# Gated cross-attention block, one core: the opening's loads, bias sums and the place of the next contexts' statistics

## What is computed

```python
x = x + tanh(g_xattn) * attention(layernorm(x), ctx)   # own layer norms and affine gains inside
x = x + tanh(g_ffn) * ffn(layernorm(x))                # W1, W2 -> round(W / (mean|W| + 1e-5)) in {-1, 0, 1}
# attention(query, context):
q, c = layer_norm(query, gq, betq), layer_norm(context, gkv, betkv)
Q, K, V = q @ Wq + bq, c @ Wk + bk, c @ Wv + bv        # 16 heads
out = softmax(Q K^T * 32**-0.5) V @ Wo + bo
```

## Time and profile before

| | |
|---|---|
| median of 3 runs | 1109.72 us |
| lowest, highest | 1107.94, 1113.02 us |
| the profiled execution's own time and span | 1107.94 and 1107.9 us |
| PE busy | 945.0 us (85%) |
| DVE busy | 798.8 us (72%) |
| ACT busy | 650.0 us (59%) |
| POOL busy | 299.1 us (27%) |

### The profile page before, as it was taken

One profiled execution on the slowest core, in us unless ns is written; L12 is line 12 of the kernel. 1 busy time (PEld: TensorE's weight loads), 2 busy tenths in 40 slices (PEclk: granted clock), 3 DMA queues, 4 the chain that ended last, 5 costly groups with the idle time before them and its releaser, 6 DMA issues.

```text
span 1107.9 us, 24975 instructions
## 1 busy us (share of the span) xinstructions
PE 945.0 (85%) x8994; PEld 721.5 (65%) x8994; DVE 798.8 (72%) x1486; ACT 650.0 (59%) x1330; POOL 299.1 (27%) x342
## 2 busy tenths in 40 slices
PE   1767769768999899889989898989989998888868
PEld 0434545556677767776778667876778677757737
DVE  2625759998797688768878679768877777788621
ACT  1744635665677457745767467745775576557611
POOL 2122035424232122404240323113240423023013
PEclk9888689869999999999999899999999999979969
DMA  7365542535022322124112402232212111320000
GB/s 233 129 189 141 139 135 74 136 93 153 14 56 57 90 79 55 44 51 131 30 26 57 137 32 55 57 86 83 55 40 56 56 43 30 71 63 1 11 27 17
DMA packets 55997, 84.05 MB, mean 76 GB/s; under 512 B 5416, under 2 KB 32488, under 8 KB 55896
## 3 DMA queue, kind: packets, MB, share of 16 engines
q1 hardware_dynamic: 49240, 65.79, 22.2%
q10 hardware_dynamic: 6656, 16.78, 5.1%
HBM read 42.20 MB, written 3.67 MB: 41 GB/s over the span
## 4 chain that ended last, share of the span: by engine, by line
PE 60%; DVE 15%; DMA 7%; issue 7%; SPq 4%; ACT 3%; POOL 2%; DVEq 0%; ACTq 0%; POOLq 0%
PE ps_fill L454 39%; PE ps_score L466 6%; PE ps_pv L495 6%; PE ps_exp L479 5%; DVE row_max L803 5%; DMA ctx_raw<-ctx_in 5%; DVE p_parts L820 3%; PE ps_fill L505 2%; SPq L368 2%; PE ps_fill L547 1%; DMA v_now<-w_q 1%; ACT h_full L716 1%; DVE row_max_parts L809 1%; PE ps_pv L592 1%; SPq L418 1%
## 5 line engine op out<-in xcount | busy, mean ns | idle before, releaser
L666 ACT ACTIVATE p_full<-ps_exp 125x448 f32<-125x448 f32 x384 | 209.4, 545 | 175.8 <-PE ps_exp L479 114.9
L820 DVE TENSOR_TENSOR p_parts<-p_full,p_parts 125x448 f16<-125x448 f32 x384 | 251.8, 658 | 2.3 <-ACT p_parts L668 2.3
L803 DVE TENSOR_REDUCE row_max<-ps_score 128x1 f32<-128x750 f32 x256 | 238.5, 932 | 13.6 <-PE ps_score L466 13.5
L668 ACT ACTIVATE p_parts<-ps_exp 125x448 f16<-125x448 f32 x384 | 209.8, 546 | 0.0
L466 PE MATMUL ps_score<-k_stack,q_stack 96*128 96x375 f16 x512 | 133.6, 344 | 89.3 <-DVE row_max L803 67.4
L479 PE MATMUL ps_exp<-q_stack,k_stack 99*125 99x224 f16 x768 | 145.0, 274 | 1.1 <-ACT p_parts L668 0.9
L479 PEld LDWEIGHTS ps_exp<-q_stack,k_stack 99*125 99x125 f16 x768 | 103.5, 145 | 31.7 <-issue 3.5
L495 PE MATMUL ps_pv<-v_now,p_parts 125*128 125x66 f16 x3072 | 121.2, 198 | 3.3 <-issue 2.7
L1116 POOL TENSOR_TENSOR h_parts<-h_full,h_parts 128x448 f16<-128x448 f32 x64 | 79.4, 1240 | 162.9 <-DVE h_parts L916 162.9
L495 PEld LDWEIGHTS ps_pv<-v_now,p_parts 125*128 125x128 f16 x3072 | 116.2, 101 | 5.6 <-issue 3.3
L466 PEld LDWEIGHTS ps_score<-k_stack,q_stack 96*128 96x128 f16 x512 | 42.4, 100 | 115.5 <-DVE row_max L803 79.8
(11 more groups left out here) (128 smaller groups left out, 1634.0 us busy)
## 6 DMA issues: line engine op xcount, KB each, us to landing
v_now<-v_stage SPq DMA_DIRECT2D x32, 386.7 KB
ctx_raw<-ctx_in SPq DMA_DIRECT2D x8, 1500.0 KB
k_stack<-k_stage_hi SPq DMA_DIRECT2D x64, 187.5 KB, 2.7
h_parts<-w1t ACTq DMA_DIRECT2D x16, 512.0 KB, 4.3
h_parts<-w2t ACTq DMA_DIRECT2D x16, 512.0 KB, 4.9
k_stack<-k_stage_lo SPq DMA_DIRECT2D x32, 187.5 KB, 3.5
x_for_q<-x SPq DMA_DIRECT2D x16, 256.0 KB, 10.8
x_residual<-x SPq DMA_DIRECT2D x16, 256.0 KB, 2.8
```

The costliest lines, as they stand in the source:

```text
L666: nc.scalar.activation(p_full[0:KR, k % 2, :], ps_exp[0:KR, k % 2, 0:2 * NQ], ACT.Exp, scale=EXP_SCALE)
L668: nc.scalar.activation(ph[0:KR, unit, :], ps_exp[0:KR, k % 2, 0:2 * NQ], ACT.Exp, scale=EXP_SCALE).then_inc(exp_done, 1)
L803: nc.vector.tensor_reduce(mx[:, h, t:t + 1], ps_score[:, :, 0:KH], AX.XY, ALU.max) \
L820: nc.vector.tensor_tensor(pl[0:KR, unit, :], p_full[0:KR, k % 2, :], ph[0:KR, unit, :], ALU.subtract).then_inc(p_split, 1)
```

## The change

It has four parts.

1. SP's list at the start: context 0 first, in three transfers of two tiles with a semaphore each (`first_loaded`), then x, then the weights. The five small loads (columns of gains and biases, gates, `bo`, `b2`) move to ACT's queue.
2. `bias_sum` takes a 128 x 128 block of the weights as stationary operand and one column of shifts as moving operand, 16 times, so the sums come out as columns in `ps_pv`; the copies by DVE and the transfer that turned them go. The third sum stands behind the transposes of OPEN.
3. In FIRST and SECOND of the tables, `stat` stands later. OPEN has no `piece_sum` and no `weight` above 7; FIRST takes them, and its `v` come before the scores.
4. SP sets the constant rows (`minus_m`) after it issued context 1, and copies q and k of batch 0 to the stacks before v.

```diff
 OPEN_WORK:
-     ("weight", 4), ("weight", 5), ("weight", 6), ("weight", 7), ("bias_sum", 0), ("bias_sum", 1),
-     ("load_pieces", 0), ("norm", 0), ("norm", 1), ("cx", 0), ("cx", 1), ("bias_sum", 2), ("norm", 2),
+     ("bias_sum", 0), ("weight", 4), ("weight", 5), ("weight", 6), ("weight", 7), ("bias_sum", 1),
+     ("norm", 0), ("norm", 1), ("cx", 0), ("cx", 1), ("norm", 2), ("norm", 3), ("load_pieces", 0), ("cx", 2),
...
+     ("xx", 1), ("bias_sum", 2), ("bias_ready", 0)],
 FIRST_WORK:
-    [("k", 4), ("stat", 0), ("piece_sum", 7), ("weight", 15), ("k", 5), ("stat", 1)],
+    [("v", 3), ("stat", 0), ("stat", 1), ("piece_sum", 9)],
+    [("v", 4), ("stat", 2), ("stat", 3), ("stat", 4)],
+    [("v", 5), ("stat", 5), ("stat", 6), ("stat", 7), ("rstd", 0), ("piece_sum", 10)],
...
+    [("norm", 6), ("mr", -1), ("norm", 7), ("cx", 5), ("piece_sum", 13), ("xx", 0), ("xx", 1),
+     ("piece_sum", 14), ("piece_sum", 15), ("tot", 0), ("threshold", 0)],
 SECOND_WORK:
-    [("q", 0), ("mr", 2), ("ternary", 1), ("q", 1), ("stat", 0), ("stat", 1), ("reload", 0), ("k", 0),
+    [None, ("reload", 6), ("mr", 5), ("ternary", 8), ("reload", 7), ("stat", 0), ("stat", 1)],
...
+            load_first_ctx()
             load_x(0, xq, x_loaded)
-            load_ctx(0)
...
-                for c in range(DC):
-                    last = pe.matmul(ps_bias[j], col[:, beta + c:beta + c + 1], raw[name][:, c, :],
-                                     start=(c == 0), stop=(c == DC - 1))
+                for m in range(DC):
+                    for c in range(DC):
+                        last = pe.matmul(ps_pv[:, 0, 4 * j + m:4 * j + m + 1], raw[name][:, c, m * P:(m + 1) * P],
+                                         col[:, beta + c:beta + c + 1], start=(c == 0), stop=(c == DC - 1))
...
+            def load_first_ctx():
+
+                rows = ctx_in[0].rearrange("(i p) d -> p i d", p=KR)
+                for j in range(3):
+                    sp.dma_start(ctx_raw[0:KR, 2 * j:2 * j + 2, :], rows[:, 2 * j:2 * j + 2, :]) \
+                        .then_inc(first_loaded[j], 16)
```

More of the change, by code:

```diff
@@ L109 @@
-    [("norm", 2), ("norm", 3)],
-    [],
-    [],
-    [("v", 3), ("norm", 4), ("bo_sum", 0), ("piece_sum", 12)],
-    [("v", 4), ("norm", 5), ("piece_sum", 13)],
-    [("v", 5), ("norm", 6), ("cx", 0), ("norm", 7), ("cx", 1), ("piece_sum", 14)],
-    [("cx", 2), ("cx", 3), ("mr", -1), ("cx", 4), ("piece_sum", 15), ("tot", 0), ("cx", 5), ("xx", 0),
-     ("threshold", 0), ("xx", 1)],
+    [("q", 0), ("piece_sum", 0)],
+    [("q", 1), ("weight", 8), ("weight", 9), ("piece_sum", 1)],
+    [("k", 0), ("weight", 10), ("weight", 11), ("k", 1), ("piece_sum", 2)],
@@ L273, in gated_block @@
         ps_fill = ctx.enter_context(nc.psum_tensor("ps_fill", [P, 2, 512], F32))
[L275 removed]
         ctx_loaded, x_loaded, xb_loaded = sem("ctx_loaded"), sem("x_loaded"), sem("xb_loaded")
+        first_loaded = [sem(f"first_loaded{j}") for j in range(3)]
         kq_landed = [sem(f"kq_landed{c}") for c in range(DC)]
@@ L392, in body @@
                     copy_v(3)
+                if stages == FIRST:
+                    sp.wait_ge(w_split, 3 * DC)
+                    sp.wait_ge(consts, 8)
+                    for row in range(SPLIT_ROWS, STACK_ROWS):
+                        sp.dma_start(k_flat[row:row + 1, :], minus_m[:, :]).then_inc(rows_set, 16)
                 if prep:
@@ L399, in body @@
                         copy_kq(c)
+                        if not attend:
+                            continue
                         if c == 1:
@@ L402, in body @@
                         if c >= 1:
-                            if attend:
-                                wait_alone(sp, pv_done, b * 16 + 4 * c)
+                            wait_alone(sp, pv_done, b * 16 + 4 * c)
                             copy_v(c - 1)
+                    if not attend:
+                        sp.wait_ge(v_split, n * 6 + 6)
+                        for c in range(DC - 1):
+                            copy_v(c)
                 if finish:
@@ L843, in stat @@
             def stat(n, j):
-                if j == 0:
-                    dve.wait_ge(ctx_loaded, n * 16 + 16)
+                if isinstance(n, int) and n == 0:
+                    if j < KT and j % 2 == 0:
+                        dve.wait_ge(first_loaded[j // 2], 16)
+                elif j == 0:
+                    dve.wait_ge(ctx_loaded, n * 16)
                 if j == KT:
```

74 lines of the change are left out of this document (28 added, 46 removed).

## The result

The changed kernel takes 1121.66 us (median of 4 runs, 1120.86 to 1122.93) beside 1111.36 for the kernel before (4 runs): ratio 1.0107, 95% interval 1.0080 to 1.0134. Timed again later beside its own variants it took 1122.56 us (6 runs) against 1106.40: ratio 1.0157, interval 1.0127 to 1.0187. It is slower; I had forecast 1097 us and 12.7 us won.

The account below looks back on a forecast made before the run. PE was taken to bound INNER, left unchanged; ahead of it, waits for context loads lay on the path. FIRST's 4.5 plus SECOND's net 8.2 gave 12.7 us off 1107.9: 1095.2, with the median 1.8 above, 1097 us; range 1088 to 1106.

Parts of the forecast that it names:

- Part 1, the loads: Opening: x's statistics end 2.4 us earlier, Wq lands at 23.9 us as before; no gain, since PE decides.
- Part 2, the bias sums: Opening, PE: first two sums take 10.1 us, the third 5.6; first q at 50 us, 1.6 us later.
- the rival of slow sums: Opening: one-column passes stay at 1.2 GHz, 0.21 us each, q at 54 us; total 1101 us; chance 0.17.
- Part 3, FIRST: No wait for context 1; norms at 102.6 us, 18.6 us from there to the end; SECOND begins 4.5 us earlier.
- SECOND's first half: Slots before 8: the wait for context 2 goes and its statistics move out; 14.3 us won.
- SECOND's second half: Later slots: 5.6 us of statistics added to DVE, the bound there; 6.1 us lost.
- the wait moves: SECOND's second half: the 10.65 us won go back entirely in four crowded slots; 1104 to 1106 us; chance 0.13.
- INNER: Loop after SECOND: losing the start's gain again there was excluded, its table being unchanged; no change in time.
- The rival that ended slower: Opening: loads of one-column passes do not overlap, 0.335 us each, q at 66 us; total 1113 us; chance 0.06.

Follow-up runs that it names:

- before_loads: Kernel before with only the new loads: context 0 first in three pieces, then x, small tensors issued by ACT; 1108.22 us, ratio 1.0025.
- before_copies: Kernel before with only FIRST's copies reordered: SP issues all 24 of q and k ahead of those of v; 1095.16 us, ratio 0.9887.

## Why the prediction was wrong

At the instruction of the table I had -12.7 us and the trace has +14.0. The 26.7 us between, by the prediction's own steps:

- **Part 1, the loads: wrong in sign.** "Its last third lands at 20.0 again, x at 21.3, Wq at 23.9": the last third was there at 22.6, x's statistics started behind its own at 23.8, Wq landed at 26.4. I had moved transfers within a fixed sum of five engines; before_loads shows that the new loads alone cost 2.3 us at Wq. Why, the runs leave open.
- **Part 2, the bias sums: the passes and the slow price right, the fast half wrong.** 10.1 us for two sums were 13.7, since a pass kept 0.21 to the end; I had let PE be fast after 5.4 us, because the old first sum was, and the new ones never brought it there: the first grant came at 63.8 us. That is the rival of slow sums, but it priced them too low as well (q at 54): with Wq late and the transposes also at the slow pace (11.8 us for 9.4), q came at 58.54 and not at 50, 8.5 us. The rule of the Trainium skill ("TensorE: Matmul & The Clock Gate", LDWEIGHTS), a load at its columns over 1.2 GHz, 107 ns for 128, fits the f32 loads of the earlier trace rows at the full clock (0.84 us for 8); the passes of the sums took twice that, 0.21 us each.
- **Part 3, FIRST: 2.7 us.** The wait for context 1 went, and from q to the norms it took 51.2 us where I had 52.6. The end behind it took 23.2 us, not 18.6: I had counted it as ACT's work with four gaps, and the ladder of scores and maxima runs through it. The rest of the difference is half a microsecond between the thresholds and the instruction of the table.
- **Part 3, SECOND's first half: size nearly right, cause wrong.** 12.5 us won for 14.3. I gave it to the moved statistics, because the chain ended in the load that they wait for. The load was late from SP's queue, and before_copies wins 10.2 us there without moving a statistic. In the changed kernel, too, it was issued at 127.4 and not at "about 115".
- **SECOND's second half: 9.7 lost for 6.1.** I priced 5.6 us of DVE work; what costs is the chain of norm, transpose, lift and split in few slots, with PE waiting and its clock at half. That was the rival "the wait moves", and its price (10.65 back) was near.
- **INNER: 10.1 us.** "I exclude because its table did not change": this step failed most plainly. Its table did not change, its place in PE's code did. 1.5 of the 10.1 us are the step in slot 11 and belong to the trace of the kernel before.

The rival that ended slower, with a chance of 0.06, had no overlap of the loads at 0.335 us; that was not what happened, passes overlapped at 0.21. The changed kernel is slower by three costs of some 10 us, of which I had one at zero.

## What to carry to other kernels

When a load is late, follow the queue that issues it back to what it waits for, before moving its user. A user moved out of the way only hands the wait to the next transfer of that queue. Count the instructions that a change adds ahead of a loop on its busiest engine, and if the time of the untouched loop moves, shift the loop's start with idle instructions before believing anything about the change itself. Small matmuls are not cheap because they have one column: price them by weight load at the slow pace, and the work behind them too.

## What the runs showed of the hardware

- This loop on PE pays 2.9 to 3.7 us at each return without a releaser, and 1.2 to 2.3 us more, plus slow matmuls behind it, when it starts at an unlucky place: 144 idle instructions cost 10 us over four returns, and 256 do not. The fetch queue moved 85 packets in the five bad traces and 80 or 81 in the thirteen good ones.
- One-column f32 matmuls with 128 x 128 weights run at 0.21 us each for 14 us on end, PE and weight loads without a gap; the first grant of the full clock came only in the q's behind them, at 63.8 us. Transposes behind them take 1.91 us for eight, 1.07 behind 512-column passes, which had the grant during the first sum. The clock column reads 1.00 in both cases, because ahead of the trace's first record it has nothing else to show; there the durations decide.
- The granted clock differs between executions where the code is the same: two stretches at half clock in FIRST, or one in batch 1, are in some traces and not in others, and go with some 3 and 1.5 us of lag. Lags of that size are read together with the clock.
- 170 semaphore increments on PE are not free: the first matmul started at 26.91 us behind "issue". With 144 it started at 22.92 us, when Wq had landed.
